# Graph network kernel: slots gathered and summed in groups of 16 instead of 8, with the end of each tile in the tile itself

## The chip, the cores and the metric

The kernel runs on one core of a Trainium2 chip. The metric is device time in microseconds (us) of one whole execution. The core has a matrix engine (TensorE, PE in the profile), a vector engine (VectorE, DVE), an activation engine (ScalarE, ACT), a general engine (GpSimd, POOL) that here mainly issues transfers with indices from memory, and SyncE (SP) that issues plain transfers.

## What is computed

Three layers of a graph network over 3125 nodes of 128 features and 103,125 edges sorted by destination, then a residual and a layer norm. Cut to what matters:

```python
for l in range(3):
    ht = jnp.einsum('nd,rdo->nro', h, W_rel[l])            # 16 relations
    h_rel = segment_sum(ht[src, etype], dst) + h @ W_loop[l] + b_rel[l]
    z = (h @ W_gat[l]).reshape(n, 4, 32)
    el, er = sum(z * attn_l[l], -1), sum(z * attn_r[l], -1)
    e = leaky_relu(el[src] + er[dst], 0.2)
    ex = exp(e - segment_max(e, dst)[dst])
    alpha = ex / segment_sum(ex, dst)[dst]
    h_gat = segment_sum(alpha[:, :, None] * z[src], dst).reshape(n, 128) + b_gat[l]
    hc = concatenate([h_rel, h_gat], 1) @ W_fuse + b_fuse
    if l == 0: hc = hc * sigmoid(concatenate([hc, mean(edge_weight)], 1) @ W_gate + b_gate)
    h = relu(hc)
out = layernorm(x + h)
```

## The kernel before

The first 270 us or so prepare: a count of edges per node, a ranking of the nodes by falling number of edges, and a table in memory with one row per node and relation (260 numbers: 128 of the message, 128 of z, 4 of the attention term el). The ranked nodes form 25 tiles of 128 nodes, one node per partition. A tile has as many slots as its node with most edges; the inputs fix them: 58, 43, 41, 40, 38, 38, 37, 36, 36, 35, 34, 34, 33, 32, 32, 31, 31, 30, 29, 28, 28, 27, 26, 24, 21, in sum 842 per layer and 2526 in all. A slot is one indirect gather, issued by GpSimd (L641): 128 rows of the table, one per partition, picked by a column of indices that VectorE staged before.

Slots are worked on in groups of 8. Each tile has a group A and a group B (its first 16 slots, indices in `stage_head`), for each further 16 another A and B (`stage_mid_A`, `stage_mid_B`), then a group t8 if the count has the bit 8, and a group t7 of up to seven slots fetched in pieces of 4, 2 and 1. For a group (`group` of the vector block, L1401 to L1449) VectorE adds `er` to the logits (`raw`), takes the running maximum (`top`, `peak`), subtracts it (`logit`), sums the messages (L1432) while ScalarE takes the exponentials (L864, L865), multiplies z by the weights (L1436) into a tile `zx` of its own, rescales what was summed so far (L1438) and sums z and denominators (L1447). It runs an online softmax, so each group needs the sums of the one before.

The order is written out by hand; there is no planner. GpSimd's `tile` issues A's eight gathers, then the store of the tile before the last, then B's, the middle ones, and, after a wait for the indices of the tail (`s_tail`), t8 and t7. The indices of the tail are staged by VectorE inside group A (`stage_tails`, L1374), those of the next tile's first 16 inside group B. What follows a tile's sums (transposes, the product with W_fuse, the gate, the next layer's table rows) is done by TensorE and ScalarE while VectorE is in the next tile's groups A and B; VectorE's own part of it (`epilogue`, `norm_statistics`) stands after the next tile's group B. Loops over tiles run per layer on each engine, with their bounds read from `tile_slots` at the top of each tile (`load_slots`, L395).

```python
group("A", stage=True, meanwhile=lambda: stage_tails(t, n, in_first), first=True)
group("B", stage=True, meanwhile=lambda: between(l, t, previous))
if previous is not None:
    epilogue(l, previous)
```

Of the kernel before, what the change touches and what calls it, by code (L numbers as in the profile page):

```python
# [23 lines left out]
def gnn_kernel(nc, x, src, dst, etype, eweight, W_rel, b_rel, W_loop, W_gat, attn_l, attn_r, b_gat,  # L40
# [23 lines left out]
    LOWER_BY = 16 * BLOCK // 2  # L64
# [11 lines left out]
    with ExitStack() as ctx:  # L76
# [28 lines left out]
        values = sb("values", [P, CLS, HB], BF16)  # L105
# [51 lines left out]
        dst_i = sb("dst_i", [EP, EC], I32)  # L157
        dst_next = sb("dst_next", [EP, EC], I32)
        src_i = sb("src_i", [EP, EC], I32)
        typ_i = sb("typ_i", [EP, EC], I32)  # L160
        lo_bf = sb("lo_bf", [EP, EC], BF16)
        hi_bf = sb("hi_bf", [EP, EC], BF16)
        lo_i = sb("lo_i", [EP, EC], I32)
        hi_i = sb("hi_i", [EP, EC], I32)
        ew = sb("ew", [EP, EC])
# [31 lines left out]
        GROUPS = dict(A=8, B=8, t8=8, t7=7)  # L197
        PIECES = dict(t4=4, t2=2, t1=1)
        GA = ("A", "B", "t8", *PIECES)
        GK = dict(GROUPS, **PIECES)  # L200
        TAIL = GA[2:]
        room = meta_nat[:].rearrange("p t f -> p (t f)")
        slots, used = {}, 0
        slots["t8"] = scratch[:, 0:8 * ROW].rearrange("p (k f) -> p k f", k=8)
        for b in ("A", "B", "t7"):
            slots[b] = room[:, used:used + GK[b] * ROW].rearrange("p (k f) -> p k f", k=GK[b])
            used += GK[b] * ROW
        for b, first in zip(PIECES, (0, 4, 6)):
            slots[b] = slots["t7"][:, first:first + GK[b]]
        assert used <= T * META and 8 * ROW <= 3 * W  # L210

        stage_head = sb("stage_head", [P, PAIR], U32)
        stage_mid = {b: sb(f"stage_mid_{b}", [P, 8], U32) for b in "AB"}
        stage_tail = {b: sb(f"stage_{b}", [P, GK[b]], U32) for b in TAIL}
        stage_hub = {b: sb(f"stage_hub_{b}", [P, GK[b]], U32) for b in GA}

        stage_id = [sb(f"stage_id{i}", [P, 1], U32) for i in range(2)]
# [5 lines left out]
        raw = sb("raw", [P, 9, H])  # L223
        leaky = sb("leaky", [P, 9, H])
        top = sb("top", [P, 1, H])
        peak = sb("peak", [P, 1, H])
        logit = sb("logit", [P, 9, H])
        zx = sb("zx", [P, 9, H, EX])
        acc = sb("acc", [P, H, EX])
        rel = sb("rel", [P, D])  # L230
        rden = sb("rden", [P, H, 1])
        hg = sb("hg", [P, H, DH])
        hr = sb("hr", [P, D])
# [913 lines left out]
        def _(dve):  # L1147
# [253 lines left out]
            def group(b, stage=False, n_slots=None, meanwhile=None, first=False):  # L1401
# [13 lines left out]
                if stage:  # L1415
                    stage_mids(b)
# [143 lines left out]
```

## Time and profile before

| | us |
|---|---|
| median of 3 runs | 4332.41 |
| lowest, highest | 4314.51, 4339.47 |
| the profiled execution | 4307.28 |
| its span, first to last instruction | 4305.7 |
| VectorE busy | 2592.4 |
| GpSimd busy | 2533.3 |
| TensorE busy | 722.6 |
| ScalarE busy | 520.0 |

No engine is busy for much more than 60% of the span. Busy times don't count register and branch instructions; a gather counts on GpSimd for the time in which it is issued, not for its transfer. Idle time in the trace is put down to what ended it; "issue" means that nothing that the profile shows was waited for.

### The profile page before, as it was taken

The page shows a single profiled execution, that of the slowest core. Times are in us where ns is not written, and L with a number is a line of the kernel's source. Part 1 is how long each engine was busy: PE and PEld are TensorE (multiplying, and loading weights), DVE is VectorE, ACT ScalarE, POOL GpSimd, SP SyncE. Part 2 cuts the span into 40 slices and gives each one's busy share as a digit, 9 for nine tenths or more (in the row PEclk, how much of TensorE's full clock was granted, in tenths as well). Part 3 has the DMA queues.
Part 4 walks back from the last instruction along what each step waited for, and adds up shares of the span by engine and source line. Part 5 has one row for each costly group of instructions (what it writes and reads, how often), then busy time and mean ns, then how long its engine had stood idle before and what let it go on. Part 6 is the DMA issues. An engine that isn't in the chain of part 4 may idle for free.

```text
span 4305.7 us, 24967 instructions
## 1 busy us (share of the span) xinstructions
PE 722.6 (17%) x1896; PEld 363.1 (8%) x1896; DVE 2592.4 (60%) x5608; ACT 520.0 (12%) x1448; POOL 2533.3 (59%) x2681
## 2 busy tenths in 40 slices
PE   7630111112112120011111122130000000000000
PEld 5310000001001010000000010010000000000000
DVE  6326666666656645665566656664756666655665
ACT  4320111111111110011111111120000000000000
POOL 0256666666666645666666656656556655665564
PEclk9765555555555555555555555555555555555555
DMA  6764444444444434434444444444233333333232
GB/s 216 259 241 87 122 133 130 129 130 128 135 137 122 144 114 84 133 103 125 124 132 124 150 122 126 147 129 110 75 82 90 91 83 80 84 87 83 74 82 55
DMA packets 152508, 517.23 MB, mean 120 GB/s; under 512 B 45704, under 2 KB 53464, under 8 KB 139680
## 3 DMA queue, kind: packets, MB, share of 16 engines
q0 software_dynamic: 132384, 452.73, 37.0%
q1 hardware_dynamic: 20096, 64.25, 4.0%
q14 instruction: 25, 0.20, 0.0%
q8 instruction: 3, 0.05, 0.0%
HBM read 351.66 MB, written 165.18 MB: 120 GB/s over the span
## 4 chain that ended last, share of the span: by engine, by line
issue 36%; DVE 32%; DVEq 12%; another core or an unknown queue 8%; PE 4%; POOL 3%; DMA 3%; ACT 1%; SPq 1%; POOLq 0%; ACTq 0%; PEldq 0%
DVE acc L1447 8%; DVE ps_rel L1432 4%; DVE zx L1436 4%; POOL meta_nat L641 3%; DVE top L1421 2%; DVEq L397 2%; PE ps_tab L959 2%; DVE zx L1438 2%; DVE raw L1418 1%; DVEq L1533 1%; DVEq L417 1%; DVE rel L1432 1%; DVEq L1408 1%; DVE logit L1430 1%
## 5 line engine op out<-in xcount | busy, mean ns | idle before, releaser
L641 POOL DMA_INDIRECT meta_nat<-table,stage_head x1200 | 1139.9, 950 | 524.3 <-issue 470.7
L1447 DVE TENSOR_REDUCE acc<-zx 128x132 f32<-128x1188 f32 (+1 forms) x348 | 766.6, 2203 | 125.0 <-remote 106.9
L641 POOL DMA_INDIRECT meta_nat<-table,stage_mid_A x384 | 364.0, 948 | 377.4 <-DVE zx L1436 256.2
L641 POOL DMA_INDIRECT scratch<-table,stage_t x312 | 296.2, 949 | 327.0 <-issue 326.7
L864 ACT ACTIVATE ps_cnt<-logit 128x36 f32<-128x36 f32 (+1 forms) x348 | 71.5, 205 | 3266.3 <-DVE logit L1430 1441.8
L641 POOL DMA_INDIRECT meta_nat<-table,stage_mid_B x384 | 364.1, 948 | 140.0 <-issue 121.7
L1432 DVE TENSOR_REDUCE ps_rel<-meta_nat 128x128 f32<-128x896 f32 (+1 forms) x234 | 441.8, 1888 | 0.0
L959 PE MATMUL ps_tab<-wrel,hT 128*128 128x512 f32 x600 | 412.1, 830 | 168.4 <-ACT rows L790 98.6
L1101 PE MATMUL ps_mix<-ident,hr 128*128 128x128 f32 x75 | 35.7, 475 | 2396.1 <-DVE hg L1465 1404.1
L1436 DVE TENSOR_TENSOR zx<-meta_nat,ps_cnt 128x1024 f32<-128x1024 f32 (+1 forms) x309 | 365.7, 1183 | 27.5 <-issue 19.6
L641 POOL DMA_INDIRECT meta_nat<-table,stage_t x246 | 233.5, 949 | 111.4 <-issue 110.8
L1101 PEld LDWEIGHTS ps_mix<-ident,hr 128*128 128x128 f32 x75 | 13.7, 182 | 2462.2 <-DVE hg L1465 1449.3
L1452 DVE COPY er_cur<-meta 128x4 f32 (+1 forms) x75 | 13.4, 179 | 343.2 <-issue 343.2
L1365 DVE COPY stage_mid_A<-ell 128x8 int32 x123 | 26.7, 217 | 269.8 <-issue 104.0
L790 ACT ACTIVATE rows<-ps_tab 128x512 f32<-128x512 f32 x300 | 171.3, 597 | 130.6 <-PE ps_tab L959 66.5
L959 PEld LDWEIGHTS ps_tab<-wrel,hT 128*128 128x128 f32 x600 | 150.5, 270 | 360.5 <-issue 192.7
L1418 DVE TENSOR_TENSOR raw<-meta_nat,er_cur 128x32 f32<-128x32 f32 (+1 forms) x309 | 62.9, 204 | 169.3 <-issue 143.1
L1432 DVE TENSOR_REDUCE rel<-meta_nat 128x128 f32<-128x1024 f32 x75 | 145.1, 1935 | 0.0
L949 PE MATMUL ps_z<-wz,hT 128*128 128x264 f32 (+1 forms) x150 | 74.5, 594 | 353.2 <-DVE hT L1481 186.8
L1421 DVE TENSOR_REDUCE top<-raw 128x4 f32<-128x36 f32 (+1 forms) x348 | 74.7, 215 | 89.7 <-remote 57.0
L891 ACT ACTIVATE rows<-ps_z 128x2112 f32<-128x2112 f32 x50 | 96.1, 1922 | 207.5 <-issue 170.0
L1107 PE MATMUL ps_mix<-hrT,wfuse 128*128 128x128 f32 x100 | 39.7, 501 | 384.4 <-ACT hgT L871 232.7
(190 smaller groups left out, 1850.6 us busy)
## 6 DMA issues: line engine op xcount, KB each, us to landing
table<-rows SPq DMA_DIRECT2D x50, 1040.0 KB
meta_nat<-table,stage_head POOLq DMA_INDIRECT x1200
meta_nat<-table,stage_mid_A POOLq DMA_INDIRECT x384
meta_nat<-table,stage_mid_B POOLq DMA_INDIRECT x384
scratch<-table,stage_t POOLq DMA_INDIRECT x312
meta_nat<-table,stage_t POOLq DMA_INDIRECT x246
meta<-meta_ranked POOLq DMA_DIRECT2D x1, 3250.0 KB
xin<-in_x SPq DMA_DIRECT2D x48, 64.0 KB, 4.5
```

Source lines behind the costliest of these rows:

```text
L397: n = eng.value_load(tile_slots[0:1, bass.ds(t, 1)], min_val=PAIR, max_val=E)
L641: pool.indirect_dma_start(out=slots[b][:, k, :], out_offset=None, in_=table[l % 2], in_offset=bass.IndirectOffsetOnAxis(ap=indices[:, k:k ...
L790: s.activation(rows[k][:, c * RC:(c + 1) * RC, 0:D], ps_tab[c % 2][:].rearrange("p (r f) -> p r f", r=RC), ACT.Copy).then_inc(s_bank[(c + ...
L891: s.activation(rows[last][:, :, D:ROW], bc(ps_z[:, 0:D + H], R), ACT.Copy)
L949: pe.matmul(ps_z[:, 0:width], hT[k][:], wz[:, l, 0:width], start=True, stop=True).then_inc(s_z_ps, 1)
L959: pe.matmul(ps_tab[c % 2][:], hT[k][:], wrel[:, l, c * RC * D:(c + 1) * RC * D], start=True, stop=True).then_inc(s_chunk[c], 1)
L1418: v.tensor_tensor(raw[:, lo:8], slots[b][:, :, 2 * D:ROW], er_cur[:].to_broadcast([P, K, H]), ALU.add).then_inc(s_raw, 1)
L1421: v.tensor_reduce(top[:, 0], raw[:, lo:9].rearrange("p k h -> p h k"), AX.X, ALU.max).then_inc(s_top, 1)
L1432: v.tensor_reduce(rel[:] if first else rel_part, slots[b][:, :, 0:D].rearrange("p k d -> p d k"), AX.X, ALU.add).then_inc(s_part, 1)
L1436: v.tensor_tensor(zx[:, lo:8, :, 0:DH], slots[b][:, :, D:2 * D].rearrange("p k (h c) -> p k h c", h=H), wgt[:, lo:8].to_broadcast([P, K, H ...
L1438: v.tensor_tensor(zx[:, 8], acc[:], wgt[:, 8].to_broadcast([P, H, EX]), ALU.mult).then_inc(s_scaled, 1)
L1447: v.tensor_reduce(acc[:], zx[:, lo:9].rearrange("p k h e -> p h e k"), AX.X, ALU.add).then_inc(s_acc, 1)
```

## The change

Groups have 16 slots. There are four buffers: H for a tile's first 16 slots, M1 and M2 for further ones in turn, T for the last up to 15, each with one more row 0. Z and denominators now lie together in the table row (per head 32 numbers of z and a place for the logit, which is set to 1.0 after it was read), so that the product is made in place in the buffer, and the running sums are copied into row 0 of the buffer and summed with the group. ScalarE takes one exponential per group, always over 17 rows. A group T always computes 15 slots and the carried row; the slots that are not fetched were cleared. The indices of the 48 slots behind the first 16 are staged in one go, for the next tile, after a tile's middle groups; those of the tail at the top of the tile itself, ahead of its first group, after a clearing of the T buffer. GpSimd waits for a tile's tail indices, issues the tail, and only then the store of the tile before. The end of a tile (the transposes, the gate, the norm) now comes in that tile, with VectorE waiting for it in the first and in the last layer. The table's rows are made in one buffer, the arrays of the first 270 us share room with M1 and M2, and W_gat is loaded with three transfers in the new order of columns.

```diff
-        GROUPS = dict(A=8, B=8, t8=8, t7=7)
-        PIECES = dict(t4=4, t2=2, t1=1)
...
+        GROUPS = dict(H=16, M1=16, M2=16, T=15)
...
+        homes = dict(H=room[:, 0:FLAT], M1=late[:, 0:FLAT], M2=late[:, FLAT:2 * FLAT], T=scratch[:, 0:16 * ROW])
...
+        def weighted(b, lo, hi):
+            return slots[b][:, lo:hi, D:ROW].rearrange("p k (h e) -> p k h e", e=EX)
+        def logits_of(b, lo, hi):
+            return slots[b][:, lo:hi, D + DH:ROW:EX]
...
# GpSimd, one tile
-                free("A")
-                gather(l, "A", stage_head[:, 0:8])
-                if not isinstance(t, int):
-                    with pool.If(t > 1):
-                        store_tile(l, last=False)
-                free("B")
-                gather(l, "B", stage_head[:, 8:16])
...
+                free("H")
+                gather(l, "H", stage_head)
                 with pool.If(in_first > 1):
...
+                    pool.wait_ge(s_mid, n_mid)
+                    free("M1")
+                    gather(l, "M1", stage_mid[:, 0:PAIR])
...
+                pool.wait_ge(s_tail, n_tail)
+                pool.reg_add(n_tail, n_tail, 1)
...
+                with pool.If(bits(pool, n, PAIR - 1) > 0):
+                    free("T")
+                    gather_tail(l, n, PAIR // 2)
+                with pool.If(t > 0):
+                    store_tile(l)
...
# ScalarE, one group
-                s.activation(wgt[:, 8 - K:9, :, 0], logit[:, 8 - K:9, :], ACT.Exp).then_inc(s_wgt, 1)
-                s.activation(zx[:, 8 - K:8, :, DH], logit[:, 8 - K:8, :], ACT.Exp).then_inc(s_wcol, 1)
+                s.activation(wgt[:, :, :, 0], logit[:], ACT.Exp).then_inc(s_wgt, 1)
...
# VectorE
+            def stage_this_tail(t, in_first):
+                v.memset(messages("T", 1, PAIR), 0.0)
+                v.memset(logits_of("T", 1, PAIR), LEAST)
+                at = dve.snap(in_first * PAIR + t * ELL, min_val=0, max_val=(T + 1) * ELL - PAIR)
+                v.tensor_copy(stage_tail[:].bitcast(I32), ell_flat[:, bass.ds(at, PAIR - 1)]).then_inc(s_tail, 1)
...
+                if not first:
+                    v.tensor_copy(slots[b][:, 0], acc[:]).then_inc(s_carried, 1)
+                    dve.wait_ge(s_carried, n_c)
+                    dve.reg_add(n_c, n_c, 1)
+                v.tensor_reduce(acc[:, 0:D], messages(b, lo, K + 1).rearrange("p k d -> p d k"), AX.X, ALU.add
+                                ).then_inc(s_part, 1)
...
-                v.tensor_tensor(zx[:, lo:8, :, 0:DH], slots[b][:, :, D:2 * D].rearrange("p k (h c) -> p k h c", h=H),
-                                wgt[:, lo:8].to_broadcast([P, K, H, DH]), ALU.mult).then_inc(s_free[b], 1)
-                v.tensor_tensor(zx[:, 8], acc[:], wgt[:, 8].to_broadcast([P, H, EX]), ALU.mult
-                                ).then_inc(s_scaled, 1)
...
+                v.tensor_tensor(weighted(b, lo, K + 1), weighted(b, lo, K + 1),
+                                wgt[:, lo:K + 1].to_broadcast([P, K + 1 - lo, H, EX]), ALU.mult).then_inc(s_product, 1)
+                dve.wait_ge(s_part, n_g)
+                dve.wait_ge(s_product, n_g)
+                v.tensor_reduce(acc[:, D:ROW], slots[b][:, lo:K + 1, D:ROW].rearrange("p k f -> p f k"), AX.X, ALU.add
+                                ).then_inc(s_acc, 1)
...
                 elif l == L - 1:
+                    norm_statistics(l, t)
...
+                stage_this_tail(t, in_first)
                 start_tile(t)
-                group("A", stage=True, meanwhile=lambda: stage_tails(t, n, in_first), first=True)
-                group("B", stage=True, meanwhile=lambda: between(l, t, previous))
+                group("H", first=True, meanwhile=lambda: stage_next_head(t))
...
+                stage_next_mid(t)
...
+                    group("T")
...
                 end_tile(t)
+                epilogue(l, t)
```

VectorE's instructions at the end of a tile of the first layer and at the top of the next one, up to the staging of the tail's indices. Before, from the reciprocal of the denominators (L1460) on:

```order
L1460 RECIPROCAL rden<-acc 128x4 [waits sums_updated]
L1461 ISA
L1461 TENSOR_TENSOR hr<-rel,meta 128x128
L1464 REGISTER_ALU [waits denominators_inverted]
L1465 TENSOR_TENSOR hg<-acc,rden 128x128
L1533 REGISTER_ALU
L1533 COMPARE_AND_BRANCH
```

and in the changed kernel, from the same instruction on:

```order
L1370 RECIPROCAL rden<-acc 128x4 [waits sums_updated]
L1371 ISA
L1371 TENSOR_TENSOR hr<-acc,meta 128x128
L1374 REGISTER_ALU [waits denominators_inverted]
L1375 TENSOR_TENSOR hg<-acc,rden 128x128
L1389 SCALAR_TENSOR_TENSOR th<-th,hc 128x128 [waits gate_ready]
L1391 TENSOR_SCALAR hT<-th 128x128 [waits gating_step]
L1392 REGISTER_ALU
L1404 ISA [waits rows_stored]
L1405 COPY stage_id<-id_u 128x1
L1461 REGISTER_ALU
L1461 COMPARE_AND_BRANCH
```

Before, the loop went on to the next tile at once, and the wait for the gate (`gate_ready`) stood behind the next tile's group B. Now it stands ahead of the branch. What comes at the top of the next tile now (`scratch` is the room of buffer T):

```order
L351 TENSOR_LOAD tile_slots
L351 ISA x2
L354 ISA
L1315 MEMSET scratch 128x15x128
L1316 MEMSET scratch 128x15x4
L1318 ISA
L1318 COPY stage_tail<-ell 128x15
L1363 ISA
L1363 COPY er_cur<-meta 128x4
```

The tail's staging moved from inside the first group to the top of the tile. GpSimd's queue in one tile of the first layer before, from the first eight gathers to the second eight:

```order
L641 DMA meta_nat<-table,stage_head 128x260 x8
L723 COMPARE_AND_BRANCH
L700 REGISTER_ALU [waits rows_ready]
L705 REGISTER_ALU [waits ids_staged]
L707 DMA table<-rows,stage_id 3200x4160
```

and now, from the last piece of the tail to the store:

```order
L619 COMPARE_AND_BRANCH
L609 DMA scratch<-table,stage_tail 128x260
L619 UNCONDITIONAL_BRANCH
L731 COMPARE_AND_BRANCH
L681 REGISTER_ALU [waits rows_ready]
L686 REGISTER_ALU [waits ids_staged]
L688 DMA table<-rows,stage_id 3200x4160
```

The store moved from behind a tile's first eight gathers to behind its tail.

## Rows read from the trace of the kernel before

**Rows 1.** The page: busy shares, the chain's engines, two costly groups (busy, mean; idle).

```profile
PE 722.6 (17%) x1896; PEld 363.1 (8%) x1896; DVE 2592.4 (60%) x5608; ACT 520.0 (12%) x1448; POOL 2533.3 (59%) x2681
...
issue 36%; DVE 32%; DVEq 12%; another core or an unknown queue 8%; PE 4%; POOL 3%; DMA 3%; ACT 1%; SPq 1%; POOLq 0%; ACTq 0%; PEldq 0%
...
L641 POOL DMA_INDIRECT meta_nat<-table,stage_head x1200 | 1139.9, 950 | 524.3 <-issue 470.7
...
L1452 DVE COPY er_cur<-meta 128x4 f32 (+1 forms) x75 | 13.4, 179 | 343.2 <-issue 343.2
```

**Rows 2.** GpSimd's timeline, three gathers: start, duration, what, idle before it.

```profile
1239.57 0.95 POOL L641 DMA_INDIRECT meta_nat<-table,stage_head  x1 [0.30 <-issue]
1248.79 0.95 POOL L641 DMA_INDIRECT scratch<-table,stage_t  x1 [8.27 <-issue]
...
3100.46 0.94 POOL L641 DMA_INDIRECT meta_nat<-table,stage_mid_A  x1 [13.42 <-DVE zx L1436]
```

**Rows 3.** Line L1452, the first vector instruction of each tile: shortest, median, longest, starts.

```profile
L1452 DVE COPY er_cur<-meta x75: 170/170/416, 259.4 to 4250.0; 128x4 f32 x72, 128x4 f32<-128x4 f32 x3
```

**Rows 4.** Timeline, a tail group's last gather and the group's first vector instruction.

```profile
1209.46 0.95 POOL L641 DMA_INDIRECT scratch<-table,stage_t  x1 [0.30 <-issue]
...
1212.40 0.19 DVE L1418 TENSOR_TENSOR raw<-scratch,er_cur 128x32 f32<-128x32 f32 x1 [3.89 <-DMA scratch<-table,stage_t]
```

**Rows 5.** VectorE's groups of instructions by form: busy us, mean ns, idle before.

```profile
L1447 DVE TENSOR_REDUCE acc<-zx 128x132 f32<-128x1188 f32 x285 | 640.8, 2248 | 107.5 <-remote 89.4 <-issue 12.8 <-DVE newton L1504 3.2
L1432 DVE TENSOR_REDUCE ps_rel<-meta_nat 128x128 f32<-128x1024 f32 x171 | 330.6, 1933 | 0.0
L1436 DVE TENSOR_TENSOR zx<-meta_nat,ps_cnt 128x1024 f32<-128x1024 f32 x246 | 297.8, 1210 | 17.7 <-issue 14.8 <-ACT ps_cnt L864 2.9
...
L1447 DVE TENSOR_REDUCE acc<-zx 128x132 f32<-128x1056 f32 x63 | 125.8, 1997 | 17.5 <-remote 17.5
L1432 DVE TENSOR_REDUCE ps_rel<-meta_nat 128x128 f32<-128x896 f32 x63 | 111.2, 1765 | 0.0
L1438 DVE TENSOR_TENSOR zx<-acc,ps_cnt 128x132 f32<-128x132 f32 x348 | 98.5, 283 | 0.0
...
L1383 DVE MEMSET meta_nat<- 128x896 f32 x75 | 60.4, 805 | 9.9
```

**Rows 6.** VectorE's timeline, first and last instruction of two groups of 8 slots.

```profile
3115.35 0.19 DVE L1418 TENSOR_TENSOR raw<-meta_nat,er_cur 128x32 f32<-128x32 f32 x1
...
3119.50 2.25 DVE L1447 TENSOR_REDUCE acc<-zx 128x132 f32<-128x1188 f32 x1
...
3132.28 0.19 DVE L1418 TENSOR_TENSOR raw<-scratch,er_cur 128x32 f32<-128x32 f32 x1 [1.82 <-DMA scratch<-table,stage_t]
...
3143.60 2.26 DVE L1447 TENSOR_REDUCE acc<-zx 128x132 f32<-128x1188 f32 x1 [2.52 <-remote]
```

**Rows 7.** VectorE's timeline, from a tile's last to the next tile's first group, twice.

```profile
1228.49 0.28 DVE L1465 TENSOR_TENSOR hg<-acc,rden 128x128 f32<-128x128 f32 x1
...
1241.26 0.19 DVE L1418 TENSOR_TENSOR raw<-meta_nat,er_cur 128x32 f32<-128x32 f32 x1 [1.23 <-issue]
...
3160.66 0.29 DVE L1465 TENSOR_TENSOR hg<-acc,rden 128x128 f32<-128x128 f32 x1
...
3162.94 0.19 DVE L1418 TENSOR_TENSOR raw<-meta_nat,er_cur 128x32 f32<-128x32 f32 x1
```

**Rows 8.** Timeline, the end of a tile on TensorE and ScalarE, first layer.

```profile
1229.09 0.42 PE L1102 MATMUL ps_mix<-ident,hg 128*128 128x128 f32 x1
...
1242.42 0.35 ACT L870 ACTIVATE hrT<-ps_mix,brel 128x128 f32<-128x128 f32 x1
...
1244.76 0.79 PE L1117 MATMUL ps_mix<-hc,wgate 128*128 128x128 f32 x2 [0.46 <-ACT hc L877]
```

**Rows 9.** VectorE's timeline, first and last instruction of a tile's norm, last layer.

```profile
3107.59 0.29 DVE L1498 SCALAR_TENSOR_TENSOR y<-ps_mix,meta 128x128 f32<-128x128 f32 x1
...
3114.78 0.46 DVE L1491 TENSOR_SCALAR yo<-y,mv,newton 128x128 f32<-128x128 f32 x1 [0.21 <-issue]
```

More of the change, by code:

```diff
@@ L238, in gnn_kernel @@
         y = sb("y", [P, D])
-        yo = [sb(f"yo{i}", [P, D]) for i in range(2)]
+        yo = sb("yo", [P, D])
         stats = sb("stats", [P, 6])
@@ L752, in tile @@
-                        with pool.Fori(0, pool.snap(now, min_val=1, max_val=BLOCK // PAIR)):
-                            for b in ("A", "B"):
-                                free(b)
-                                gather_hub(l, b)
-                pool.wait_ge(s_tail, n_tail)
-                pool.reg_add(n_tail, n_tail, 1)
-                for is_hub, run in ((pairs > BLOCK // PAIR, lambda b: gather_hub(l, b)),
-                                    (pairs <= BLOCK // PAIR, lambda b: gather(l, b, stage_tail[b]))):
-                    with pool.If(is_hub):
-                        tail_groups(pool, n, lambda b: (free(b), pieces(pool, n, run) if b == "t7" else run(b)))
@@ L763, in _ @@
-            n_head = counter(pool, "pool_head", 1)
-            n_mid = {b: counter(pool, f"pool_mid_{b}", 2) for b in "AB"}
-            n_tail = counter(pool, "pool_tail", 2)
+                        with pool.Fori(0, groups_of_block()):
+                            free("M2")
+                            hub_indices(stage_hub[:], PAIR)
+                            gather(l, "M2", stage_hub)
+                    hub_indices(stage_tail[:], PAIR - 1)
+                with pool.If(bits(pool, n, PAIR - 1) > 0):
+                    free("T")
+                    gather_tail(l, n, PAIR // 2)
@@ L773, in _ @@
                     pool.wait_ge(s_stored, 16 * (1 + l * T))
-                tile(l, 0)
-                with pool.Fori(1, T) as t:
+                with pool.Fori(0, T) as t:
                     tile(l, t)
-                store_tile(l, last=False)
                 store_tile(l, last=True)
@@ L926, in _, with tile @@
+            def tile(l, t):
+                n = act.value_load(tile_slots[0:1, bass.ds(t, 1)], min_val=PAIR, max_val=E)
+                act.reg_add(n_groups, n, PAIR - 1)
+                act.reg_alu(n_groups, n_groups, PAIR.bit_length() - 1, ALU.logical_shift_right)
+                with act.Fori(0, act.snap(n_groups, min_val=1, max_val=E // PAIR + 1)):
+                    group()
+                transposed(l)
+                fused(l)
+                gate_and_table(l, t)
             act.wait_ge(s_bload, 16 * (5 + 3 * L))
@@ L933, in _ @@
             for l in range(L):
-                tile(l, 0, None)
-                with act.Fori(1, T) as t:
-                    tile(l, t, t - 1)
-                transposed(l)
-                fused(l)
-                gate_and_half_table(l, last=True)
-                rest_of_table(l, T - 1, last=True)
+                with act.Fori(0, T) as t:
+                    tile(l, t)
         @block.tensor
```

440 lines of the change are left out of this document (183 added, 257 removed).

## The prediction

> **What bounds the kernel now.** I read the page first. No engine is busy for more than 60% of the span: VectorE 2592 us, GpSimd 2533, and the chain of waits names "issue" with 36% and VectorE with 32% [rows 1]. So neither a busy engine nor memory sets the time; what each tile waits for does. GpSimd's timeline gives the floor: gathers stand 0.95 us with 0.30 before each [rows 2], 1.25 us a slot, so 2526 slots take 3158 us; 75 stores at about 1.3 us more (taken like a gather) add 98. The tiles run from 259.4 to the last one's start at 4250.0 [rows 3], 3991 us. GpSimd is thus without work for some 735 us in it, 9.7 us a tile, in gaps such as 8.27 and 13.42 us [rows 2]. The change can win at most those, and loses where they grow.
>
> A gap is a wait for a tail's indices or a free buffer. In a tile of 30 slots before (the first layer, around 1241 us) the circle is: from the first `raw` at 1241.26 [rows 7] to the first tail gather at 1248.79 [rows 2] 7.5 us; 13 further gathers 16.3; landing, from the last gather's issue at 1209.46 to `raw` at 1212.40, 2.9 [rows 4]; the tail group with the two products behind it 6.6 (a fast group of 6.4, below, a little shorter for seven slots, and the end's 0.6); the top 12.8. Sum 46.1. In the last layer the norm stands in VectorE's queue too: 5.4 us more (below), 51.5.
>
> The trace has two speeds. A group of 8 takes 6.4 us (3115.35 to 3119.50+2.25) or 13.6 us (3132.28 to 3143.60+2.26), with the same instructions equally long and the time between them [rows 6]; a tile's end to the next `raw` takes 2.3 us (3160.66) or 12.8 (1228.49) [rows 7]. GpSimd resumed at 3100.46 [rows 2]: 15 us later a group is fast, 32 us later slow. I take it that such a stretch begins 28 us after gathers resume and ends 4 us after they pause; both are choices within what these rows allow. The Trainium skill (NOTIFIC — the notification-queue block, "Overflow: three behaviours, one of which stalls the engine") says that the block's inner pipeline holds its producers back rather than lose records, and can so throttle an engine. That would fit stretches that come with many gathers. The median of the runs shown, 25 us above the profiled execution, does not show that running without a profile is faster, so I give the rule no price of its own.
>
> **The change, part by part.**
>
> *A group of 16.* VectorE's sum of messages goes from 1765 ns at 7 slots to 1933 at 8 [rows 5], 0.17 a slot; 17 rows cost 1.93+9×0.17=3.5 us. The product of 1024 elements takes 1210 ns [rows 5], 2244 elements 2.6. The sum over z and denominators goes from 1997 to 2248 ns for one more slot [rows 5], 0.25; with nine more that is 4.5. In place in rows of 260 the slope may be that of the messages, which gives 3.8. Bounds 3.5 to 4.5; I take 3.7, as the messages' sum reads rows of that stride. The copy of 260 running sums is not in the trace: the product of 132 takes 283 ns [rows 5], so 0.28 to 0.56, taken 0.4. Small steps 1.2 (from 6.4 less 1.9, 1.2, 0.3 and 2.2, with something to spare since one is gone). Sum 11.3 us; for H, which has no carried row, 10.4; for T, always 16 rows, 10.8. Two groups of 8 cost 12.8, so a full pair saves 1.5 to 2.4 us of VectorE, but a T of one slot costs 10.8 where a small tail cost 5.8. Per layer there are 64 groups where there were 116. In a slow stretch a group of 8 pays +7.2; for one of 16 I put +9, since its sum waits for the carried copy and for the product one after the other, so about 20 us, and a pair saves 7 there.
>
> *The top.* Clearing T is 15×128 elements: 896 take 805 ns [rows 5], so 1.8 us with the small one, and 0.2 for the copy: 2.0 us ahead of the tail's gathers, which before stood inside group A. In exchange the wait of 7.5 us from `raw` to the first tail gather goes. The clearing is hidden nowhere: GpSimd waits for it once H, and M1 if there is one, are issued.
>
> *The end in the tile.* VectorE now waits for TensorE and ScalarE. From `hg` at 1228.49 [rows 7] to the matmul at 1229.09+0.42, 1.0 us; from `hrT` at 1242.42 to the gate's product, 1244.76+0.79, 3.1 [rows 8]; a tanh of about the 0.35 of hrT, two vector steps of some 0.3 and hops: 5.5 us in the first layer. In the last layer some 3.3 us to the fused product, and the norm from 3107.59 to 3114.78+0.46 [rows 9], 7.7 less the z sum of 2.2 that stands between, 5.4: in sum 8.7. The second layer waits for nothing. This was covered by groups A and B before; now it is on VectorE's line, and in tiles of few slots on that of the next tail. Queued behind VectorE's wait are `stage_id`, the next top and so the next tail's indices, for which GpSimd waits.
>
> *The store* moved behind the tail. It waits for the previous tile's rows, which TensorE and ScalarE finish in this tile's H group, about 10 us after the top; the tail and H cover it, except at tails of one or two slots. I cost it at nothing; without cover it is 2 us in two or three tiles of a layer.
>
> **Per kind of tile.** Clock from the resumption of the gathers.
>
> - 21 to 31 slots, 10 a layer, n = 30: 13 gathers and landing 19.2, group T to 30.0, its last 2 us in a stretch, so 31.5. First layer: end 0.6, chain 5.5, its hops slow (+1.2 to 2.6 each) until the gathers have paused (14 and 16 gathers and a store, 38.8, plus 4 = 43): 44.5, top 2.3 and clearing 2.0, 48.8 against 46.1, +2.7. Second layer: the top itself is slow, 46.5, +0.4. Last: 8.7 instead of 5.5, with some of it slow, 53.5 against 51.5, +2. Ten each: +51.
> - 33 to 43 slots, 12 a layer, n = 36: VectorE's groups 10.4+11.3+10.8=32.5 against 31.4 (four of 6.4, one of 5.8), so nothing is saved; GpSimd's floor 36×1.25+1.3=46.3. H and M1 are ready, T ends at 33, with its stretch 38; end, chain and top are slow until 50 (46.3+4): 56, 51.5, 59 in the three layers. Before I put 54, 52, 56 by the same rule. Bounds −5 (the buffers of 48 slots bring it near the floor) to +6 (no pause ends a stretch); taken +2, 36 times, +72.
> - 32 slots, 2 a layer: no T, so two groups saved: −3, 6 times, −18.
> - 58 slots, 1 a layer: eight groups become four, mostly in a slow stretch: four times 13.6×2−20 is −29, of which I count −17 a layer, since gathers of 58 slots, 72.5 us, cover some of it: −50.
>
> The transitions between layers and the first 260 us I leave as they are. Sum +55: 4307+55=4362 for the profiled execution, and with the 25 us to the median, 4387; I say 4390.
>
> **The rivals.**
> 1. *Faster: the stretches thin out.* VectorE's instructions in groups fall from 348 groups of some 11 to 192 of some 10, to about half; if the stretches go by that and not by gathers alone, they shrink. Without any, a tile of 30 slots takes 2.0+19.2+10.8+0.6+5.5+2.3=40.4 (46.1 before), those of 36 the floor of 46.3 (54): about −6 and −7.5 on 30 and 36 tiles, −450, −540 with the others. A third of the way from +55 to there is −140: 4190. For: the slow time stands between instructions. Against: the gathers, which seem to start it, are as many. It decides if half the groups at the end of a tile are fast.
> 2. *Faster: the tops were loading code.* 343 us of idle time stand before L1452, the first instruction after the loop's branch, put down to "issue" [rows 1]: 4.6 us a tile. The changed program is far shorter. If most of it goes, and the rest is as forecast but for small hops, 4390−290=4100. Against: group 3132.28 is slow in straight code and 3160.66 crosses the branch in 2.3 us [rows 6, 7]. The Trainium skill (Runtime: NRT & Kernel Launch, "Instruction fetch mechanics") says that a taken branch outside the two pages at hand waits for a fetch.
> 3. *Slower yet: permanent stretches.* With four buffers GpSimd hardly pauses in the tiles of 33 to 43; a stretch is then never ended and the whole end, chain and top are slow: +6 instead of +2, +144: 4530. For: a gap of the kind of 8.27 us is what ended them. Against: then VectorE is late and makes a gap again.
> 4. *No change.* The kinds cancel: with tiles of 36 at +0.5 instead of +2 (−54) the sum is +1, and the median 4333. For: the forecast's +2 is small beside its bounds.
>
> **Numbers.** Forecast 0.36 (own range 4350 to 4460), rival 1 0.22, rival 2 0.08, rival 3 0.20, rival 4 0.14. A measurement of this kernel can tell about 0.5%, 22 us, from no change. Faster 0.30 (1 and 2), same 0.14, slower 0.56. The range takes rival 1 nearly whole and rival 3 whole: 4120 to 4620.
>
> **What the changed profile would show.** The z sum 3.5 to 4.5 us, the sum of messages near 3.5, the product 2.6, the carry copy under 0.6; fast groups 11, slow ones about 20; `hg` to the staging of the tail about 10 us in the first and last layer, 4 fast or 13 slow in the second; gaps on GpSimd before the first tail gather of 8 to 14 us in short tiles; the tile of 58 slots some 17 us shorter. I am wrong if fast groups are above 13 us, if slow stretches are gone, or if the second layer gains as little as the first: the chain would then not be what costs.

## The result, and the profile after

The changed kernel took 4194.42 us (median of 4, 4189.75 to 4196.33) against 4335.94: ratio 0.968, 95% interval 0.966 to 0.970. I had forecast 4390, slower. The figure is that of rival 1, 4190. A *stretch* below is what the prediction called a slow stretch: a time in which VectorE's instructions are as long as ever, and what lies between them is slow.

The page of the changed kernel: busy shares, then GpSimd's gathers into buffer H and some of VectorE's groups (busy us, mean ns; idle us before them and what ended it).

```profile
PE 713.2 (17%) x1896; PEld 354.9 (8%) x1896; DVE 2589.9 (62%) x3225; ACT 458.4 (11%) x944; POOL 2524.9 (60%) x2681
...
L609 POOL DMA_INDIRECT meta_nat<-table,stage_head x1200 | 1137.4, 948 | 711.7 <-issue 563.0
...
L1352 DVE TENSOR_TENSOR meta_nat<-meta_nat,ps_cnt 128x2112 f32<-128x2112 f32 x75 | 176.3, 2350 | 366.4 <-issue 272.7
L1356 DVE TENSOR_REDUCE acc<-meta_nat 128x132 f32<-128x2112 f32 x75 | 290.3, 3871 | 7.7
...
L1346 DVE TENSOR_REDUCE acc<-meta_nat 128x128 f32<-128x2048 f32 x75 | 281.9, 3759 | 0.0
L1315 DVE MEMSET scratch<- 128x1920 f32 x75 | 124.3, 1658 | 241.6 <-issue 241.6
```

VectorE is as busy as before [rows 1], with 3225 instructions instead of 5608; the gain is in the time between them. The idle time at the tiles' tops was 343.2 us [rows 1] and is 241.6. New are 366 us of idle time ahead of the product of group H (L1352). The first vector instruction that both kernels have in each tile, the source view's line (shortest, median, longest, starts):

```profile
L1363 DVE COPY er_cur<-meta x75: 158/160/425, 267.5 to 4149.9; 128x4 f32 x75
```

The tile loop takes 3882.4 us where it took 3990.6 [rows 3], -108. From the same starts, us a tile, mean over the tiles of a kind:

| slots | forecast, layers 1 / 2 / 3 | measured |
|---|---|---|
| 21 to 31 | +2.7 / +0.4 / +2 | -1.8 / -1.5 / -1.5 |
| 33 to 43 | +2 | +2.0 / -2.2 / -0.8 |
| 32 | -3 | -5.8 / -5.0 / -2.7 |
| 58 | -17 | -10.4 / -16.7 / +0.6 |

These means move by some us between executions: from c_before to c_after, a second pair, the tiles of 21 to 31 slots gave -2.9 / -2.0 / -4.1. VectorE's timeline of the changed kernel in the first layer, a group H's product with the 13.44 us waited ahead of it, then the same tile's group T and its end:

```profile
749.41 2.35 DVE L1352 TENSOR_TENSOR meta_nat<-meta_nat,ps_cnt 128x2112 f32<-128x2112 f32 x1 [13.44 <-ACT ps_cnt L829]
...
768.04 0.26 DVE L1328 TENSOR_TENSOR raw<-scratch,er_cur 128x60 f32<-128x60 f32 x1
...
775.76 3.86 DVE L1356 TENSOR_REDUCE acc<-scratch 128x132 f32<-128x2112 f32 x1
...
779.99 0.28 DVE L1375 TENSOR_TENSOR hg<-acc,rden 128x128 f32<-128x128 f32 x1
784.65 0.29 DVE L1389 SCALAR_TENSOR_TENSOR th<-th,hc 128x128 f32<-128x128 f32 x1 [4.38 <-ACT th L848]
784.98 0.23 DVE L1391 TENSOR_SCALAR hT<-th 128x128 f32<-128x128 f32 x1
...
787.00 1.66 DVE L1315 MEMSET scratch<- 128x1920 f32 x1 [1.67 <-issue]
```

The group T takes 11.6 us, from 768.04 to 779.62, where I had 38 - 22 = 16 for it in a stretch; end, chain and top follow at their quick pace, 7.0 us from the start of hg to the clearing. It is no exception: of the 69 groups T of this trace 68 take 11.6 to 11.7 us, and the longest 13.5. One tile alone would prove little, as the gathers had paused for 13 us just before, until 756.59, which by my rule too ends a stretch. What is slow here is ScalarE, ahead of group H's exponential. ScalarE's timeline in the same tile, the last two of the four copies of the previous tile's table rows, and then the exponential:

```profile
742.25 0.60 ACT L755 ACTIVATE rows<-ps_tab 128x512 f32<-128x512 f32 x1 [5.01 <-remote]
747.84 0.60 ACT L755 ACTIVATE rows<-ps_tab 128x512 f32<-128x512 f32 x1 [4.99 <-remote]
...
749.08 0.23 ACT L829 ACTIVATE ps_cnt<-logit 128x68 f32<-128x68 f32 x1 [0.47 <-issue]
```

The copies start 5.6 us apart, though TensorE had ended the last product that they copy at 739.4.

The trace also holds each engine's register, branch and semaphore steps, called steps below; with the instructions they make up its records. In a stretch many a step lasts 0.70 us and not some 0.04. VectorE has 11,078 records of all kinds in the kernel before and 6596 now; its steps of 0.70 us (0.69 to 0.71 counted), strung together where the next starts within 4 us, span 704 us of the kernel before and 329 of this one. ScalarE has no step of 0.70 us in the changed kernel: its slowness lies between its records, and what it waits for is not shown.

### The profile page after: what moved, and what is told of

It is laid out like the page before. It is cut to its first block and busy times, and to the rows that moved or that the text cites. A ratio compares the mean times of both kernels' runs of the same rounds, so it can differ in the third digit from the quotient of the medians.

```text
span 4194.8 us, 18977 instructions
## 1 busy us (share of the span) xinstructions
PE 713.2 (17%) x1896; PEld 354.9 (8%) x1896; DVE 2589.9 (62%) x3225; ACT 458.4 (11%) x944; POOL 2524.9 (60%) x2681
## 5 line engine op out<-in xcount | busy, mean ns | idle before, releaser
L609 POOL DMA_INDIRECT late<-table,stage_mid x768 | 726.6, 946 | 234.0 <-issue 231.2
L609 POOL DMA_INDIRECT scratch<-table,stage_tail x558 | 527.5, 945 | 314.8 <-issue 314.5
L1352 DVE TENSOR_TENSOR meta_nat<-meta_nat,ps_cnt 128x2112 f32<-128x2112 f32 x75 | 176.3, 2350 | 366.4 <-issue 272.7
L1356 DVE TENSOR_REDUCE acc<-meta_nat 128x132 f32<-128x2112 f32 x75 | 290.3, 3871 | 7.7
L1346 DVE TENSOR_REDUCE acc<-meta_nat 128x128 f32<-128x2048 f32 x75 | 281.9, 3759 | 0.0
L1315 DVE MEMSET scratch<- 128x1920 f32 x75 | 124.3, 1658 | 241.6 <-issue 241.6
L1356 DVE TENSOR_REDUCE acc<-scratch 128x132 f32<-128x2112 f32 x69 | 266.5, 3862 | 7.1
L1346 DVE TENSOR_REDUCE acc<-scratch 128x128 f32<-128x2048 f32 x69 | 258.7, 3750 | 10.7 <-issue 2.1
L1356 DVE TENSOR_REDUCE acc<-late 128x132 f32<-128x2244 f32 x48 | 195.5, 4072 | 5.0
L1346 DVE TENSOR_REDUCE acc<-late 128x128 f32<-128x2176 f32 x48 | 189.7, 3952 | 8.9 <-remote 2.7
L1352 DVE TENSOR_TENSOR scratch<-scratch,ps_cnt 128x2112 f32<-128x2112 f32 x69 | 161.7, 2343 | 0.0
L1352 DVE TENSOR_TENSOR late<-late,ps_cnt 128x2244 f32<-128x2244 f32 x48 | 119.0, 2480 | 0.0
```

What stands on the lines that cost most here:

```text
L609: pool.indirect_dma_start(out=slots[b][:, k, :], out_offset=None, in_=table[l % 2], in_offset=bass.IndirectOffsetOnAxis(ap=index, axis=0)) ...
L1315: v.memset(messages("T", 1, PAIR), 0.0)
L1346: v.tensor_reduce(acc[:, 0:D], messages(b, lo, K + 1).rearrange("p k d -> p d k"), AX.X, ALU.add).then_inc(s_part, 1)
L1352: v.tensor_tensor(weighted(b, lo, K + 1), weighted(b, lo, K + 1), wgt[:, lo:K + 1].to_broadcast([P, K + 1 - lo, H, EX]), ALU.mult).then_in ...
L1356: v.tensor_reduce(acc[:, D:ROW], slots[b][:, lo:K + 1, D:ROW].rearrange("p k f -> p f k"), AX.X, ALU.add).then_inc(s_acc, 1)
```

## The experiments

The first set of runs brought what I had not looked for: the kernel before took 3654 us in it and not 4336, and no engine had a step of 0.70 us. The later sets fell on either of these two levels of time, and each has its own time of the kernel before. "With stretches" below is before at 4312 to 4353, "without" before at 3648 to 3654. The level does not go with the chip: c_before (4355) and h_before (3648) ran on the same one.

| run | before, same set | this | ratio, 95% interval |
|---|---|---|---|
| c_after, with | 4353 | 4207 | 0.9667 (0.9641 to 0.9692) |
| g_after, without | 3651 | 3782 | 1.0358 (1.0341 to 1.0376) |
| f1_sync_steps, with | 4312 | 4798 | 1.112 (1.110 to 1.115) |
| f2_vector_steps, with | 4312 | 4612 | 1.069 (1.066 to 1.071) |
| f3_spaced, with | 4312 | 5774 | 1.338 (1.335 to 1.341) |
| e1_sync_steps, without | 3654 | 3780 | 1.034 (1.032 to 1.036) |
| e2_vector_steps, without | 3654 | 3785 | 1.035 (1.033 to 1.037) |
| e3_exp_first, without | 3654 | 3785 | 1.035 (1.034 to 1.037) |
| e4_tail_early, without | 3654 | 3685 | 1.008 (1.006 to 1.010) |
| e5_both, with | 4353 | 4269 | 0.980 (0.978 to 0.983) |
| e7_all, with | 4353 | 4162 | 0.956 (0.954 to 0.959) |
| g_all, without | 3651 | 3799 | 1.041 (1.039 to 1.042) |
| e6_defer, without | 3651 | 3800 | 1.041 (1.039 to 1.043) |

**Both kernels at both levels.**

> The kernel before, unchanged, for its trace where no slow stretches are: in the four runs so far VectorE had not one register step of 0.70 us, and the kernel before took 3654 us, not 4336. Theory S (the slow stretches are the whole difference between the two levels): if it takes about 3654 again, no step of 0.70 us; if about 4336, some 700 us of them. Ratio 1.00.

> The changed kernel, unchanged, beside the kernel before on the same chip. Theory S: without slow stretches it takes 3775 to 3790, since the runs with 20 more steps a group and with steps on SyncE, that cost nothing by themselves, took 3785 and 3780: ratio 1.034, slower. With slow stretches 4194, ratio 0.968. Rival: the ratio stays near 0.97 at either level, and each of the three edits cost some 6% by itself.

> The kernel before, for its trace where no slow stretches are, if the chip has none: no VectorE step of 0.70 us, a group of 8 in 6.4 us throughout, the top in 2.3, and GpSimd without a wait of more than 2 us in most tiles, since 3650 is near the 3256 us of issuing with the 270 us ahead of it and the layers' ends. Otherwise as c_before.

c_before took 4355 (ratio 1.001) with 518 VectorE steps of 0.70 us, c_after 4207 with 221, and h_before and g_after have none. For the kernel before theory S fits in size too: strung together as above, c_before's slow steps span 703 us, and 4355 - 3648 is 707. In the changed kernel they span 270 us of 4207 - 3782 = 425; the rest shows elsewhere, above all as the wait ahead of group H's product: 366.4 us in the first trace, and in g_after 20.4.

```profile
L1352 DVE TENSOR_TENSOR meta_nat<-meta_nat,ps_cnt 128x2112 f32<-128x2112 f32 x75 | 176.2, 2350 | 20.4 <-ACT ps_cnt L829 20.4
```

The rival of c_after (0.97 at either level) falls. The source view of the load at a tile's top, VectorE's queue, shortest, median and longest ns: the kernel before with and without stretches (runs before and h_before), then the changed one (after and g_after).

```profile
L397 DVEq TENSOR_LOAD <-tile_slots x75: 2/690/1080, 258.2 to 4246.8; - x75
```
```profile
L397 DVEq TENSOR_LOAD <-tile_slots x75: 311/322/958, 273.0 to 3591.6; - x75
```
```profile
L351 DVEq TENSOR_LOAD <-tile_slots x75: 2/310/1397, 264.0 to 4147.2; - x75
```
```profile
L351 DVEq TENSOR_LOAD <-tile_slots x75: 299/311/329, 279.8 to 3732.7; - x75
```

The same load has a median of 690 ns in the kernel before with stretches, and 310 in the changed one: at least half of its tops are quick. Without stretches the change costs: the pages of h_before and g_after, shares of the chain of waits.

```profile
POOL 47%; issue 27%; DVE 8%; DMA 8%; PE 4%; POOLq 3%; DVEq 1%; SPq 1%; ACT 0%; ACTq 0%; PEldq 0%
```
```profile
issue 30%; POOL 26%; DVE 24%; PE 7%; DMA 6%; DVEq 3%; POOLq 2%; ACT 1%; SPq 1%; ACTq 0%; PEldq 0%
```

In the kernel before GpSimd has the largest share there (47%); in the changed one VectorE has nearly as much as GpSimd (24 and 26%). Per tile, from the ends of hg in both traces: 21 to 31 slots 39.1 / 36.5 / 42.8 us in the three layers against 36.8 / 36.1 / 36.7; 33 to 43 slots 48.3 / 48.2 / 49.6 against 47.6 each. That is 88+39 of the 134 us between the two loops, 84 of it in the first and last layers' short tiles, where VectorE's chain at the end of a tile stands ahead of the tail's staging; e4 below tests that.

**Steps on an engine that nobody waits for (e1_sync_steps, f1_sync_steps).**

```python
+            turns = counter(sp, "sp_turns", 0)
+            sp.wait_ge(s_rows, T + 1 + T)
+            with sp.Fori(0, 5000):
+                sp.reg_add(turns, turns, 1)
```

> The changed kernel, in which SyncE, idle by then, also runs 12,800 register additions in a loop of 1600 turns from the start of the second layer on; nothing waits for it. The first and last layers are the control. Theory A (the slow stretches are a shared budget: every step of any engine and every packet of a gather takes from it): the second layer, 1259 us between the first vector instructions of its first tile and the third layer's, becomes at least 60 us longer, VectorE's steps of 0.70 us grow in it, and the other two layers stay within 10 us. Theory B (each engine's own steps and the gathers alone decide): all three layers stay within 10 us.

> The changed kernel with a loop of 5000 turns on SyncE (two steps each, 0.25 us a turn, so 1250 us without slow stretches) from the start of the second layer on; nothing waits for it. In the run e1_sync_steps only 1600 turns of two steps were left of what was written, about 400 us. Where the kernel before takes about 4350 (slow stretches): theory A (all engines' steps and the gathers' packets take from one budget) says that the second layer's tiles become 60 us or more longer in sum, to 4270 or more; theory B (each engine for itself) says 4207. Where the kernel before takes 3654: 3785 by both.

e1 fell on the level without stretches and took 3780 (1.034). f1: the source view of SyncE's loop and of VectorE's first instruction of a tile.

```profile
L477 SPq ALU_OP  x5000: 1/33/1401, 1567.7 to 4792.2; - x193
```
```profile
L1367 DVE COPY er_cur<-meta x75: 152/160/413, 270.7 to 4154.8; 128x4 f32 x75
```

The 4798 us are SyncE's own: its loop, 1250 us long if quick, ended at 4792, long after the last tile. The tile loop took 3884.1 us, as in the changed kernel (3882.4). The second layer, in which SyncE made 1788 more steps, took 1263.9 us against 1258.9: 5 more, where theory A wanted 60 or more. Its tiles of a kind were the same within 0.4 us, but for the single one of 58 slots (0.7 shorter). Theory A falls, and theory B stands: SyncE's steps made none of VectorE's slower. SyncE shows the pace: its first 138 steps, from 1567.7 on, were quick; between 1700 and 2000 us it made 214, one in 1.40 us; from 4165 on, with the gathers over (the last one at 4161.8), all were quick.

**More steps on VectorE (e2_vector_steps, f2_vector_steps).**

```python
+                with dve.Fori(0, 10):
+                    dve.reg_add(idle_steps, idle_steps, 1)
```

> The changed kernel with 20 register additions on VectorE's queue behind each group's sum of messages (3840 in all, about as many steps as the change took away). At 0.07 us each they take 1.4 us while the sum runs 3.8 us, so in fast stretches they cost nothing. Theory A (the number of steps feeds the slow stretches, as rival 1 had it): 0.70 us steps on VectorE come back to 500 us or more in sum (329 in the changed kernel, 704 before) and the time grows by 80 to 250 us to 4275 to 4440. Theory C (the stretches go by the gathers alone, and the gain came from fewer waits for landing): below 4230.

> The changed kernel with a loop of 10 turns (two steps each) on VectorE's queue behind each group's sum of messages: 3840 steps beside the 6596 that VectorE has now (11,078 before). In e2_vector_steps the additions written out had vanished from the program. One loop takes 2.5 to 3 us beside a sum of 3.8 us, so where no slow stretches are it costs nothing or nearly: 3785. Where they are (before at 4350): theory A (the number of steps feeds them and pays for them) says 100 to 300 us more than 4207, and VectorE's steps of 0.70 us from 221 to over 800; theory C (stretches go by gathers, and steps cost only where VectorE is waited for; here they mostly hide behind nothing) says below 4240.

In e2 the 20 additions were gone from the built program (6596 VectorE records, as without them), so it is the changed kernel (3785, 1.035). f2: 4612 where the changed kernel would be at 0.9667 × 4312 = 4168, so +443 us for 4032 more records, 0.11 us each. Steps of 0.70 us: 926. Against f1, the changed kernel's work in the same set, its tile loop is 415 us longer (4299.0 and 3884.1), 0.10 each. Its quickest groups take the same 11.3 and 12.1 us, so quick steps cost nothing beside the sum. Theory A has the direction and the steps (over 800), and theory C falls; the size is above A's 100 to 300 us. Taken back from 11,078 to 6596 at that price it would be 493 us; the stretches' cost fell from 707 to 425 us, by 282. Why by less is not shown; one reading is that not every removed step stood where it was waited for.

The traces with stretches also show when one begins. Counted from the first gather behind a pause of over 4 us to VectorE's first step of 0.70 us (where that came at least 8 us later), the median is 82 records and 25.8 us in the kernel before, 73 records and 32.8 us in the changed one, and 67 records and 18.6 us in f2. The number of records stays near the same, and the time goes with the pace at which VectorE spends them. The spread is wide in the changed kernel: the middle half lies between 30 and 76 records.

**Fewer gathers per us (f3_spaced).** A clearing and a wait for it ahead of each gather.

> The changed kernel with a small clearing (128x64, of an array that nobody reads any more) and a wait for it ahead of each gather, which widens GpSimd's step of 1.25 us a gather by my estimate to 1.4 to 1.5. Where slow stretches are (before at 4350, changed 4207): theory D (they fill while gathers come at one in 1.25 us and drain when fewer come) says that they nearly vanish, VectorE's steps of 0.70 us from 221 to below 60, and that the time is that of the floor, 2526 times 0.15 to 0.25 above 3785: 4100 to 4400. Theory E (they come with any gathering) says that they stay, and 4207 plus most of the same 380 to 630: above 4500. Where none are: 4100 to 4400.

GpSimd's timeline, and the same load at the tile's top:

```profile
699.94 0.17 POOL L612 MEMSET zeros_bf<- 128x64 bf16 x1
700.90 0.95 POOL L617 DMA_INDIRECT late<-table,stage_mid  x1 [0.79 <-POOL zeros_bf L612]
701.85 0.17 POOL L612 MEMSET zeros_bf<- 128x64 bf16 x1
```
```profile
L352 DVEq TENSOR_LOAD <-tile_slots x75: 301/311/871, 262.8 to 5712.8; - x75
```

A gather came every 1.91 us, not 1.4 to 1.5: my estimate of the edit was wrong, and so the time: 5774 is far above theory D's range, and decides nothing between the two. The count of slow steps decides: on the chip and in the set of runs where f1 and f2 had stretches, no step of VectorE or GpSimd lasted 0.70 us. The level was there in this execution too: SyncE had 14 such steps between 189 and 251 us, ahead of the tiles, as in the changed kernel, and none in g_after. Theory D holds; where between 1.25 and 1.91 us the limit lies was not tried. The edit also spreads VectorE's own 6596 records over a longer loop (5449 us instead of 3882), so for VectorE alone it does not part the gathers' rate from its own; but GpSimd made 10,465 records instead of 5412, and none was slow either.

**The exponential ahead of the copies (e3_exp_first).** ScalarE's table rows of a tile behind the next tile's first exponential.

```python
+                group()
+                if previous is not None:
+                    table_rows(l, previous)
```

> The changed kernel with ScalarE's copies of a tile's table rows moved from ahead of the next tile's first exponential to behind it, nothing else. In the changed kernel VectorE stands 366 us ahead of the product of group H (L1352), for the exponential that is queued behind those copies (13.4 us in the tiles of 36 slots of the first layer). Theory 1 (this wait is on the path): it falls below 60 us, the tiles of 33 to 43 slots in the first layer go from 57.3 to about 48, and the whole to 4000 to 4080. Theory 2 (GpSimd's store and free buffers end last anyway): the wait goes but comes back as waits for landing and for the store, and the whole stays above 4150.

Without stretches the wait was small already (20.4 us in g_after), so 3785 says nothing on theory 1. e5 bears on it, together with a second edit.

**The tail's staging behind hg (e4_tail_early, g_tail_early, h_tail_early).**

```python
                 end_tile(t)
+                if following is not None:
+                    stage_tail_of(following)
                 epilogue(l, t)
```

> The changed kernel with buffer T's clearing and the tail's indices of the next tile moved from the top of that tile to right behind hg, ahead of VectorE's wait for the gate or the fused product. Theory 1 (the tail's staging is what GpSimd waits for): GpSimd's gaps before tail gathers shrink by 2 to 7 us a tile, the time falls by 80 to 200 us, most in the first and last layer. Theory 2 (in the tiles of 33 to 43 slots VectorE's own queue with the wait for the exponential sets the pace): only the 2 us of clearing that hides behind the chain is won, in the first and last layer, 40 to 100 us, and the gaps move to another place.

3685, 3679 and 3676, all without stretches: 100 us less than e2 and 104 less than g_after, each in its own set. The short tiles go to 36.4 / 36.4 / 36.8 us from 39.1 / 36.5 / 42.8, so the gain is in the first and last layers, as both theories had it, and its size stands in theory 1's range and at the upper end of theory 2's: the run shows that the tail's staging was on the path, and does not part the two. With stretches it was never seen alone.

**Both, and the end put back (e5_both, e7_all, g_all, e6_defer).** e7 has all three, e6 the exponential and the end.

```python
                 group("H", first=True, meanwhile=lambda: stage_next_head(t))
+                if previous is not None:
+                    epilogue(l, previous)
```

> The changed kernel with both the tail's staging right behind hg and ScalarE's table copies behind the next tile's first exponential. Without slow stretches the first edit gave about -98 us (3685 against 3783) and the second nothing, so 3685. With slow stretches the wait of 366 us ahead of the product of group H goes too: below 4050.

> As the one before, and the epilogue (gate step, norm, stage_id) back behind the next tile's group H, as it was in the kernel before behind group B. Theory: without slow stretches GpSimd's issuing already sets the pace in nearly all tiles, so it gains at most 20 us on 3685. With slow stretches it takes the chain of 5 to 8 us a tile off VectorE's line in the first and last layer: 50 to 200 us below the version without it.

> The changed kernel with the end of a tile undone: VectorE's gate step, norm and stage_id behind the next tile's group H, ScalarE's copies of the table rows behind the next tile's first exponential. Groups of 16, buffers and the tail's staging as changed. Theory G (the groups' fewer steps pay, the end in the tile costs): where the kernel before takes about 4350, at least 60 us below the changed kernel's 4207; where it takes 3654, 40 to 100 us below the changed kernel's 3785. Theory H (the end in the tile pays too, as fewer steps are in flight at once): slower than the changed kernel.

VectorE's groups, changed kernel (above, 366.4 and 241.6), then e5_both, then e7_all:

```profile
L1360 DVE TENSOR_TENSOR meta_nat<-meta_nat,ps_cnt 128x2112 f32<-128x2112 f32 x75 | 176.0, 2347 | 0.0
L1323 DVE MEMSET scratch<- 128x1920 f32 x75 | 124.3, 1658 | 199.1 <-issue 199.1
```
```profile
L1360 DVE TENSOR_TENSOR meta_nat<-meta_nat,ps_cnt 128x2112 f32<-128x2112 f32 x75 | 175.9, 2345 | 0.0
L1323 DVE MEMSET scratch<- 128x1920 f32 x75 | 124.3, 1658 | 191.7 <-issue 191.7
```

e5 took the whole wait of 366 us away and was 62 us slower than the changed kernel (4269 and 4207): VectorE's steps of 0.70 us rose from 221 to 691, and the tiles of 33 to 43 slots in the last layer from 58.7 to 64.8 us. My expectation (below 4050) failed. A reading that fits, argued and not shown: while VectorE waits it spends no steps, so the wait had been paying for the quick ones behind it. A rival stands beside it: the tail's staging with its own load of the bounds gives VectorE 422 more records (7018), which at f2's price of 0.11 us would be 46 of the 62 us. No run parts the two. With the end put back (e7) 107 us come back, 4162, the best time with stretches, although it has 6999 records, 403 more than the changed kernel; so the number of records does not set the time alone. e6 was not seen there. Without stretches the end behind the next group H, with the exponential moved, costs: g_all is 120 us above g_tail_early, where I had expected it level with the kernel before. GpSimd's stores, of the table's rows and of the last layer's output, and what they waited for, g_tail_early and g_all:

```profile
L688 POOL DMA_INDIRECT table<-rows,stage_id x50 | 48.8, 976 | 75.8 <-ACT meta L763 61.2 <-issue 14.6
L694 POOL DMA_INDIRECT out<-yo,stage_id x25 | 25.5, 1019 | 35.4 <-DVE stage_id L1406 28.1 <-issue 7.3
```
```profile
L688 POOL DMA_INDIRECT table<-rows,stage_id x50 | 48.9, 978 | 157.4 <-ACT meta L763 132.7 <-DVE stage_id L1413 14.8 <-issue 10.0
L694 POOL DMA_INDIRECT out<-yo,stage_id x25 | 25.5, 1019 | 80.4 <-DVE stage_id L1413 75.2 <-issue 5.3
```

What is stored now comes later than the tail, and the store, queued ahead of the next tile's gathers, holds them up: GpSimd's idle time ahead of the stores grows by 82 and 45 us, together about the 120.

> The changed kernel beside the other three on one chip. Ratio to the kernel before 0.967 where that takes about 4350, 1.035 where it takes 3654 (by e2_vector_steps, whose additions had vanished from the program, so that it was the changed kernel).

> The changed kernel with the tail staged behind hg. Where the kernel before takes 3654: 3685 again. Where it takes 4350 it adds some 6 steps a tile to VectorE's queue but lets GpSimd start the tail 5 to 8 us earlier; e5_both, which has it and the exponential first, was 62 us above the changed kernel there. If the tail's staging did that, 4230 to 4270; if the exponential did, 4100 to 4180.

> The three edits together (e7_all). Where the kernel before takes 4350: 4162 again, ratio 0.956. Where it takes 3654: GpSimd's issuing sets the pace of nearly every tile, so 3640 to 3690, which is level with the kernel before.

> e6_defer again: the changed kernel with the end of a tile behind the next tile's group H. Where the kernel before takes 3650, 3800 again. Where it takes 4350 (changed 4207): theory G (the groups' fewer steps pay, the end in the tile costs) says below 4150; theory H (the end in the tile pays as well) above 4207.

> e4_tail_early again. Where the kernel before takes 3650, 3680 again. Where it takes 4350: 4100 to 4180 if the earlier tail pays there too and it was the moved exponential that cost e5_both its 62 us, 4230 to 4270 if not.

h_defer and h_tail_early gave 3799 (1.042) and 3676 (1.008): the repeats fell on the level without stretches. Whether the end in the tile pays or costs with stretches stays undecided for that edit alone; without them theory G failed, which wanted 40 to 100 us less than 3785: e6's 3800 is 18 us above g_after.

## Why the prediction was wrong

- *What bounds the kernel.* Right as far as it went: no engine, but waits of VectorE and GpSimd, and two speeds. I took the second speed for a constant of the kernel; it is not there in half the sets of runs. (735 us over 75 tiles are 9.8 a tile, not 9.7, which changes nothing.)
- *When a stretch begins.* **This step failed.** I had "28 us after gathers resume", whatever the engine has done, and so gave the changed kernel's ends, chains and tops the same slow stretches. f3 shows stretches gone where gathers come less densely; f2, and the count of records at which a stretch begins, show that the engine's own steps decide, and f1 that SyncE's do not. The changed kernel has 4482 fewer records on VectorE, and its groups T end quick (68 of 69) where I had them slow in the tiles of 33 to 43 slots. I priced its stretches at 595 us (+55 against -540); they cost 425. This is rival 1, against which I wrote that the gathers "are as many". Its sign, half the groups at the end of a tile quick, was a poor one: in the kernel before 64 of the 75 already took less than 8 us.
- *A group of 16.* Near: sum of messages 3.76 us (3.5), product 2.35 (2.6), z sum 3.87 (3.7; bounds 3.5 to 4.5), carry copy 0.30 (0.4; [rows 5] gave 0.28 to 0.56), clearing 1.66 (1.8), T 11.6 (10.8), H 11.3 at its quickest (10.4, without the staging in it).
- *The end in the tile.* The forecast was for tiles with stretches and missed there (table above). Between h_before and g_after, without them, the short tiles' differences lie near it in two layers, which is partly luck: first layer +2.3 (+2.7), second +0.4 (+0.4), last +6.1 (+2, too low). From hg to hT it took 5.2 us in the timeline above (5.5).
- *Missed.* ScalarE is slow in stretches as well, and its copies now stand ahead of group H's exponential: 366 us, a term that I had at nothing. The first layer's tiles of 33 to 43 slots came out at the forecast +2.0, but by this wait and not by a slow T.
- *The sum without stretches*, given under rival 1 for the changed kernel: 4307 - 540 + 25 = 3792, measured 3782. The total is partly luck, since from the kernel before with stretches to the changed one without, the tiles of 21 to 31 slots win 4.7 us (6 forecast) and those of 33 to 43 win 8.1 (7.5). What I never worked out at that level was the kernel before, 3648.
- *Rival 2* (loading code at the tops): in the kernel before, idle time ahead of 72 of the tops is 319.9 us with stretches and 96.2 without, with the same loop and branches, so the branch alone is not what costs. *Rival 3* fell: no stretch was permanent, as the groups T show.
- The Trainium skill's rule (NOTIFIC — the notification-queue block, "Overflow: three behaviours, one of which stalls the engine") would fit records that pile up for each engine while the gathers' packets come. That is a reading: no run here shows it. Against it I argued from the median, which cannot tell, since each run comes with a recorded span. Whether the stretches are there when nothing is recorded is therefore open, and so is what a slow step waits for and what sets the level from one set of runs to the next.

## What to carry to other kernels

Before a difference is worked out from slow stretches, look whether they are there in each run, by the length of register steps: here the same change is 3.3% faster with them and 3.6% slower without. With the stretches, 4032 more steps on VectorE cost some 0.1 us each (f2), so fewer and longer instructions can win there even at equal busy time; without them they bought nothing, and the end of the tile in the tile cost. And taking a large wait away may win nothing (e5): look at what the engine does in the time that it gets back.

## What the runs showed of the hardware

One program took 4355 and 3648 us on one chip at different times (c_before, h_before). In the slow level a register step can last 0.70 us instead of some 0.04. SyncE, only stepping, made one step in 1.40 us while gathers came every 1.25 us, after 138 quick ones (f1); at one gather in 1.91 us no step of VectorE or GpSimd was slow (f3). VectorE's first slow step came at a median of 67 to 82 records behind the gathers' start, after 18.6 to 32.8 us. 1788 more steps of SyncE in a layer left VectorE's time there unchanged within 5 us (f1). ScalarE's copies of a tile's table rows started up to 5.6 us apart in that level (64 of 150 gaps over 5 us in the changed kernel's trace), and at most 1.7 us apart without it (g_after).
